# A graph attention layer: the third key form summed on VectorE and GpSimd instead of TensorE

## The reference

```
h = relu(layernorm(x));  mx = masked_x
S = (mx @ Wlq) @ (h @ Wlk).T / 16;  S = where(adj, S, -1e9)
g = (mx @ Wgq) @ (mean(h) @ Wgk).T / 16;  e = mx @ Wes
m = max(rowmax(S), g, e);  den = sum(exp(S - m)) + exp(g - m) + exp(e - m)
res = exp(S-m)/den @ (h @ Wlv + blv) + exp(g-m)/den * (mean(h) @ Wgv + bgv)
      + exp(e-m)/den * (mx @ Wev + bev)
out = x + max(res, mx)
```

## Time and profile before

| | |
|---|---|
| median of 3 runs | 729.83 us (729.6 to 729.88) |
| the profiled execution | 729.67 us, its span 727.8 us |
| PE, matmuls | 721.6 us busy, 99% |
| PE, weight loads | 513.1 us, 70% |
| DVE | 566.9 us, 78% |
| ACT | 532.3 us, 73% |
| POOL | 433.2 us, 60% |
| granted TensorE clock | 1.0 of full speed over the span |

### The profile page before, as it was taken

One profiled execution on the slowest core, in us unless ns is written; L12 is line 12 of the kernel. 1 busy time (PEld: TensorE's weight loads), 2 busy tenths in 40 slices (PEclk: granted clock), 3 DMA queues, 4 the chain that ended last, 5 costly groups with the idle time before them and its releaser, 6 DMA issues.

```text
span 727.8 us, 15215 instructions
## 1 busy us (share of the span) xinstructions
PE 721.6 (99%) x5344; PEld 513.1 (70%) x5344; DVE 566.9 (78%) x1349; ACT 532.3 (73%) x709; POOL 433.2 (60%) x300
## 2 busy tenths in 40 slices
PE   8999999999999999999999999999999999999998
PEld 7677566667766777676767676676777776676798
DVE  6975988777887797878887887878878787876545
ACT  6885967858677777776878687678767777777690
POOL 4779889455465455556545655565556545644584
PEclk9999999999999999999999999999999999999999
DMA  9783777869779888988878797989888798888797
GB/s 301 133 179 76 161 154 150 158 136 215 159 158 177 171 157 150 205 156 173 171 166 159 153 205 138 193 159 180 172 168 163 148 209 148 176 172 178 137 183 152
DMA packets 364764, 121.93 MB, mean 168 GB/s; under 512 B 324752, under 2 KB 364688, under 8 KB 364688
## 3 DMA queue, kind: packets, MB, share of 16 engines
q1 hardware_dynamic: 364144, 120.44, 81.8%
q10 hardware_dynamic: 544, 0.52, 0.2%
HBM read 36.57 MB, written 4.19 MB: 56 GB/s over the span
## 4 chain that ended last, share of the span: by engine, by line
PE 87%; POOL 3%; issue 3%; DVE 3%; ACT 2%; DMA 1%; DVEq 0%; SPq 0%; POOLq 0%; ACTq 0%
PE ps_u L1153 13%; PE ps_u L1157 13%; PE ps_u L1155 13%; PE ps_x L1031 7%; PE ps_x L1029 7%; PE ps_x L1030 7%; PE ps_q L953 4%; PE ps_v L1029 3%; PE ps_v L1031 3%; PE ps_v L1030 3%; POOL p_base L627 2%; PE ps_w L1029 2%; PE ps_w L1030 2%; PE ps_w L1031 2%; PE ps_q L1219 1%
## 5 line engine op out<-in xcount | busy, mean ns | idle before, releaser
L627 POOL TENSOR_TENSOR p_base<-s,p_base 128x1024 f16<-128x1024 f32 x112 | 242.3, 2164 | 229.1 <-ACT p_base L830 224.4
L1155 PE MATMUL ps_u<-v_rows,pT_base 128*128 128x256 f16 x944 | 257.3, 273 | 0.0
L1157 PE MATMUL ps_u<-v_rows,pT_base 128*128 128x256 f16 x944 | 257.3, 273 | 0.0
L1153 PE MATMUL ps_u<-v_rows,pT_base 128*128 128x256 f16 x944 | 257.3, 273 | 0.0
L793 ACT ACTIVATE bias<-adj,big 128x1024 f32<-128x1024 uint8 x127 | 156.5, 1236 | 130.8 <-DVE bmax L1522 128.9
L806 ACT ACTIVATE s<-s,negm,invc 128x1024 f32<-128x1024 f32 x128 | 157.0, 1226 | 8.8 <-DVE negm L1578 8.8
L830 ACT ACTIVATE p_base<-s 128x1024 f16<-128x1024 f32 x122 | 129.0, 1057 | 4.8 <-DMA pT_base<-p_base 0.9
L1153 PEld LDWEIGHTS ps_u<-v_rows,pT_base 128*128 128x128 f16 x944 | 92.3, 98 | 52.0
L1155 PEld LDWEIGHTS ps_u<-v_rows,pT_base 128*128 128x128 f16 x944 | 92.4, 98 | 51.9
L1522 DVE CUSTOM_DVE_ANT_0 s<-ps_x,bias 128x512 f32<-128x512 f32 x128 | 87.3, 686 | 47.1 <-PE ps_x L1031 43.0
L1157 PEld LDWEIGHTS ps_u<-v_rows,pT_base 128*128 128x128 f16 x944 | 92.4, 98 | 10.7
(11 more groups left out here) (255 smaller groups left out, 1315.4 us busy)
## 6 DMA issues: line engine op xcount, KB each, us to landing
adj<-adj SPq DMA_DIRECT2D x64, 256.0 KB, 3.2
pT_base<-p_base SPq DMA_TRANSPOSE x234, 3.2
s<-x SPq DMA_DIRECT2D x7, 512.0 KB, 7.9
f32q<-mx SPq DMA_DIRECT2D x14, 256.0 KB, 3.6
xm<-x SPq DMA_DIRECT2D x14, 256.0 KB, 3.0
xm<-mx SPq DMA_DIRECT2D x14, 256.0 KB, 3.6
out<-t_sb SPq DMA_DIRECT2D x14, 256.0 KB, 2.6
mxT_f<-mxT SPq DMA_DIRECT2D x4, 256.0 KB, 3.1
```

Source lines behind the costliest of these rows:

```text
L627: nc.gpsimd.tensor_tensor(p_rows(u)[:, 1], s32[:, p % NS, u % 2], p_rows(u)[:, 0], ALU.subtract).then_inc(s_plo, 1)
L1153: nc.tensor.matmul(acc, turn[:, 0, j], v_rows[:, kc, 0:D], start=opens, stop=False, skip_group_check=True)
L1155: nc.tensor.matmul(acc, turn[:, 0, j], v_rows[:, kc, D:2 * D], start=False, stop=False, skip_group_check=True)
L1157: done = nc.tensor.matmul(acc, turn[:, 1, j], v_rows[:, kc, 0:D], start=False, stop=end, skip_group_check=True)
```

## The change

`eye16`, its making on ACT, `keys_t3_sum`, `keys_t3_high` and `keys_t3_low` go. Two new functions of the same name `keys_t3` make the same sums from the float16 blocks in SBUF, with the float32 scratch `tw[:, 0]` that POOL's other key forms used before: an addition, two subtractions, the rounding to float16 and the subtraction of the rounded part, five instructions of 128x512 each. The first stands on DVE for groups 0 and 1, in periods 10 and 11. The second stands on POOL for groups 2 and 3, in its periods 12 and 14. The waits of PE that guarded `ps_q` and `eye16` go too; `p7`'s wait for T3 of its group stays.

```diff
-        eye16 = sb("eye16", [P, 2, P], F16)
...
+            def keys_t3(g):
+
+                pool.wait_ge(s_p7, PC - NG + g + 1)
+                pool.wait_ge(s_t3, g)
+                forms(twv[:, 0], plain(g, 1, 1, 0), plain(g, 1, 1, 1), ALU.add)
+                forms(twv[:, 0], twv[:, 0], plain(g, 0, 1, 0), ALU.subtract)
+                forms(twv[:, 0], twv[:, 0], plain(g, 0, 1, 1), ALU.subtract)
+                split(twv[:, 0], plain(g, 0, 1, 0), plain(g, 0, 1, 1), s_t3)
...
                     keys_t4((p - 3) // 2)
+                if p in (PC, PC + 2):
+                    keys_t3((p - PC) // 2 + 2)
...
-            act.wait_ge(s_const, 4)
-            for k in range(2):
-                nc.scalar.activation(eye16[:, k], ident, ACT.Copy, scale=1.0 - 2.0 * k).then_inc(s_eye, 1)
...
-                if p in (PC - 2, PC):
-                    keys_t3_high(p - PC + 2)
-                    keys_t3_high(p - PC + 3)
...
-                if n == PC // NG + 1:
-                    pe.wait_ge(s_t3, NG)
...
-            def keys_t3_sum(g):
-
-                if g < 2:
-                    pe.wait_ge(s_qf, PC - 3)
-                else:
-                    pe.wait_ge(s_c2, 2)
-                for k, (c, hl) in enumerate(((1, 0), (1, 1), (0, 0), (0, 1))):
-                    last = nc.tensor.matmul(ps_q[:, g % 2, :], eye16[:, 1 - c], plain(g, c, 1, hl), start=k == 0,
-                                            stop=k == 3)
-                last.then_inc(s_t3sum, 1)
...
                         for b in range(2):
-                            if p == PC - 2 and t:
-                                keys_t3_sum(b)
                             classic(p, t, b)
...
-                    if p == PC:
-                        keys_t3_sum(2)
-                        keys_t3_sum(3)
...
-            def keys_t3_low(g):
-                dve.wait_ge(s_t3hi, g + 1)
-                nc.vector.tensor_tensor(plain(g, 0, 1, 1), ps_q[:, g % 2].rearrange("p (j q) -> p j q", q=P),
-                                        plain(g, 0, 1, 0), ALU.subtract).then_inc(s_t3, 1)
+            def keys_t3(g):
+
+                dve.wait_ge(s_t4, NG)
+                dve.wait_ge(s_p7, PC - NG + g + 1)
+                if g:
+                    dve.wait_ge(s_t3, g)
+                at = tw[:, 0].rearrange("p (j q) -> p j q", q=P)
+                nc.vector.tensor_tensor(at, plain(g, 1, 1, 0), plain(g, 1, 1, 1), ALU.add).then_inc(s_t3sum, 1)
+                for hl in range(2):
+                    dve.wait_ge(s_t3sum, 4 * g + hl + 1)
+                    nc.vector.tensor_tensor(at, at, plain(g, 0, 1, hl), ALU.subtract).then_inc(s_t3sum, 1)
+                dve.wait_ge(s_t3sum, 4 * g + 3)
+                nc.vector.tensor_copy(plain(g, 0, 1, 0), at).then_inc(s_t3sum, 1)
+                dve.wait_ge(s_t3sum, 4 * g + 4)
+                nc.vector.tensor_tensor(plain(g, 0, 1, 1), at, plain(g, 0, 1, 0), ALU.subtract).then_inc(s_t3, 1)
...
                     out12(p)
+                    if p == PC - 2:
+                        keys_t3(0)
...
                     out22(p)
-                    if p == PC - 2:
-                        keys_t3_low(0)
-                        keys_t3_low(1)
+                    if p == PC - 1:
+                        keys_t3(1)
...
                         add12(p)
-                    if p == PC:
-                        keys_t3_low(2)
-                        keys_t3_low(3)
```

More of the change, by code:

```diff
@@ L221, in build @@
         s_t1, s_t2, s_t4, s_t3, s_tw = (sem(n) for n in ("s_t1", "s_t2", "s_t4", "s_t3", "s_tw"))
-        s_t3sum, s_t3hi, s_eye = (sem(n) for n in ("s_t3sum", "s_t3hi", "s_eye"))
+        s_t3sum = sem("s_t3sum")
         s_bias = sem("s_bias")
@@ L830, in p_high @@
                 nc.scalar.activation(p_rows(u)[:, 0], s32[:, p % NS, t], ACT.Copy).then_inc(s_phi, 1)
-            def keys_t3_high(g):
-                act.wait_ge(s_t3sum, g + 1)
-                nc.scalar.activation(plain(g, 0, 1, 0), ps_q[:, g % 2].rearrange("p (j q) -> p j q", q=P), ACT.Copy
-                                     ).then_inc(s_t3hi, 1)
             def mean_rows():
@@ L1160, in p_times_v @@
                         done.then_inc(s_pv, 1)
-            def keys_t3_sum(g):
-                if g < 2:
-                    pe.wait_ge(s_qf, PC - 3)
-                else:
-                    pe.wait_ge(s_c2, 2)
-                for k, (c, hl) in enumerate(((1, 0), (1, 1), (0, 0), (0, 1))):
-                    last = nc.tensor.matmul(ps_q[:, g % 2, :], eye16[:, 1 - c], plain(g, c, 1, hl), start=k == 0,
-                                            stop=k == 3)
-                last.then_inc(s_t3sum, 1)
             def es_values(n):
-                if n == 0:
-                    pe.wait_ge(s_t3, 2)
                 if n < QH:
@@ L1279, in _ @@
                 if b == NB - 1:
-                    pe.wait_ge(s_eye, 2)
                     pe.wait_ge(s_gev, 3)
```

## The result

The changed kernel takes **732.23 us** (median of 5 runs, 731.73 to 733.32) where the kernel before takes 729.73 (5 runs, 729.47 to 729.88): a ratio of 1.0037, with a 95% interval of 1.0026 to 1.0048. It is slower by 0.37%, more than the 0.2% that a measurement of this kernel can tell from none. Forecast were 734.4 and slower; the range, 727.2 to 736.6, holds the time. The profiled execution took 733.22 us, with a span of 731.4.

What follows compares the result with a forecast made beforehand. TensorE's matmuls cover 99% of the span, but from period 13 to 19 a ring of VectorE, ScalarE and GpSimd sets the pace. Sum: -3.45 + 3.45 + 3.2 + 1.4 = +4.6 us, so 734.4 us, range 727.2 to 736.6.

Steps and rivals of the forecast that it cites:

- TensorE's 3.45: Periods 10 and 12: 16 matmuls at 0.215 us go, taking 3.45 us of work off TensorE.
- VectorE's string to `add11(12)`: Periods 10 and 11: VectorE's added forms and blocks by GpSimd make `p6(12)` start at about 149.9, 1.7 us later.
- The ring's 3.2 at `out12(13)`: Periods 12 and 13: the pace-setting ring of VectorE, ScalarE and GpSimd gets 3.2 us late, bounds 1.2 to 4.4.
- `keys_t3(3)`'s 1.4: Period 14: GpSimd's 6.0 us form where it idled 4.62 makes `p_low(20)` and `p_low(21)` 1.4 us later.
- The gain kept: Rival, chance 0.18: VectorE's ten instructions mostly slip between GpSimd's, `add11(12)` done by 145.9; 727.6 to 726.4 us.
- Even: Rival, chance 0.22: part of the lead survives at `p6(12)`, and GpSimd's forms take it back; 729.8 give or take 1.4.
- More lost: Rival, chance 0.10: both `p_low` block, `row_max` meets three instructions, the lag reaches `p7(15)`; 5.8 + 1.4, 737 us.
- (1): Sign in the changed profile: TensorE has a gap of several microseconds before `p6(12)`, released by `add11`.
- (2): Sign: VectorE's `keys_t3` instructions much longer than 0.68 us in two or three places, each ending with one of GpSimd's.
- (3): Sign: the steps of `row_max` around 155 us take over 1 us each.
- (4): Sign: `p_low(20)` on GpSimd has no idle time before it.
- (5): Sign: TensorE's next gaps stand in periods 14 to 19, before `p5`, released by `out12`.

Runs made afterwards that it cites:

- e3: Changed kernel with all four forms left out, VectorE's and GpSimd's, an instruction of two elements signalling in their place: 725.52 us, ratio 0.9947.
- e5: Changed kernel with `keys_t3(0)` moved behind `out22(10)`: 732.53 us, ratio 1.0040.
- e4: Changed kernel with ten idle matmuls of 128x512 into a free bank just ahead of `p6(12)`: 731.81 us, ratio 1.0031.
- e1: Changed kernel without GpSimd's two forms (groups 2 and 3): 731.94 us, ratio 1.0033, six runs in two clusters.
- e2: Changed kernel without VectorE's forms (groups 0 and 1): 726.93 us, ratio 0.9966.
- e10: Changed kernel with groups 0, 1 and 3 summed on TensorE and only group 2 on GpSimd: 728.08 us, ratio 0.9981.
- e8: Groups 0 and 1 on TensorE, 2 and 3 on GpSimd, group 3's three additions one period earlier, against the changed kernel: 728.29 us, ratio 0.9983 to before.
- e11: Changed kernel without VectorE's forms, each of GpSimd's two forms replaced by memsets that read nothing: 727.75 us, ratio 0.9974.
- e9: Changed kernel with each of VectorE's ten instructions given one operand in PSUM and two inputs, values junk: 727.91 us, ratio 0.9977.
- e6: Changed kernel with groups 0 and 1 summed on TensorE as before the change, 2 and 3 on GpSimd: 728.30 us, ratio 0.9984.
- e7: Changed kernel with groups 0 and 1 kept on VectorE, groups 2 and 3 summed on TensorE as before the change: 731.81 us, ratio 1.0032.

## Why the prediction was right and wrong

**TensorE's 3.45: right.** `e3` shows 3.4 at `p6(12)` and 3.65 to 4.0 at the end.

**VectorE's string to `add11(12)`: right, by a sum of parts that were each a little off.** Forecast were `out22(11)` ended at 143.0, `add11(12)` at 149.1 and `p6(12)` at 149.9, 1.7 late; measured are 143.8, 149.40 and 150.13, 1.96 late. `keys_t3(0)` lost about 4.0 us to `p_low(11)` and the next, where 2.8 were put; `keys_t3(1)` lost 1.0 to `mx_low(4)`, where 1.1 were. The rounding takes 0.43 us, not the 0.68 that the sum used. The estimate of about 0.3 less per group, which the prediction drew from the Trainium skill (VectorE: DVE Perf Modes, Mode 2×_2P), is borne out by the row: 0.43 against 0.69.

What was not seen is that TensorE waits in three places. The change puts five instructions ahead of `out21(10)` and `out22(10)`, whose banks TensorE's product at 135.78 wants. For the time this is nothing, since the last wait decides; `e5` removes the first gap and the time doesn't fall.

**The ring's 3.2 at `out12(13)`: this step failed.** In `e4`, the change without the fall of the clock, `out12(13)` starts at 166.19, 1.44 later than the 164.75 of before. Two things were put too high. `row_max` was to lose 3.6 us and lost 1.5 there (0.74 and 1.08 for two steps of 0.16), in the profiled changed kernel 1.0. (The 4.8 us that the forecast draws from it does not come out of its terms either: 1.7 at `p6(12)` and 3.6, less the idle time of 0.26, are 5.0.) And "one block of 2.1 us" behind `out11(13)`, by `p_low(17)`, did not come: from `out11(13)` to `out12(13)` the kernel before takes 1.69 us, `e4` 1.70, the changed one 1.71. `out11(13)` is late along with everything else, so `p_low(17)` has ended when its small followers run. The error was to move one engine's instructions by their lateness and leave the other's where the trace of before had them. The rows had shown that such an instruction, when it meets one of GpSimd's, loses the whole of it; they did not show that it will meet one. In the profiled execution the lateness at `out12(13)` is 2.69; the 1.25 above `e4` are the clock.

The path was another as well. In `e4`, `out12(12)` comes 3.23 late and so does `p_low(16)` (160.26), which ends at 162.39, 2.1 us before `out11(13)` starts. 3.23 is less than the 3.9 that the forecast had to spare: by its path, through the mask and `p_low(16)`, `out11(13)` would not be late at all. It is 1.43 late because `add22(13)` waits for TensorE, and TensorE is late since `p6(12)`. Timeline of VectorE, the first row before, the others `e4` (`q_rows` in period 13, `add22(13)` ahead of it, `out12(13)`):

```profile
159.78 2.08 DVE L1444 TENSOR_TENSOR cqs<-cq,mu 128x2 f32<-128x2 f32 x1
...
159.78 0.69 DVE L1545 TENSOR_TENSOR bias<-ps_v,bias 128x512 f32<-128x512 f32 x1 [0.60 <-PE ps_v L1026]
...
161.11 1.30 DVE L1413 TENSOR_TENSOR rtrue<-rmax,mu 128x2 f32<-128x2 f32 x1
...
166.19 0.69 DVE L1502 CUSTOM_DVE_ANT_0 s<-ps_v,bias 128x512 f32<-128x512 f32 x1
```

`add22(13)` is 1.93 late (157.85 before). `q_rows` behind it is held up for 1.1 us by `p_low(16)`, where before it was held up for 1.9 by `p_low(17)`, and so 0.8 of the 1.93 is won back; some 0.3 is lost again in idle time that shows no releaser. The block that the forecast added was in the trace of before already, ahead of `out11(13)`.

**`keys_t3(3)`'s 1.4: right in size.** `e4` less `e1` at a clock of 1.000 gives 1.3 at `p5(19)` (222.29 against 220.99) and 1.0 by the times (731.81 against 730.77), `e2` less `e3` 1.4 at the end, all for both of GpSimd's forms together; `p_low(20)` follows the form after 0.16 us of idle time, and `e10` shows that taking this form off shortens the stretch between `p6(12)` and `p5(19)` by 1.35. That it comes from GpSimd's length is what `e8` and `e11` leave standing.

**The sum.** +1.44 at `out12(13)` and +1.3 would be 2.7; `e4` has 2.47 at `p5(19)` and 2.3 at the end. Read from TensorE the 2.47 are 1.92 at `p6(12)` and, in `e4`, gaps of 0.47 and 0.84 before `p5(15)` and `p5(19)` where one of 0.91 stood. The runs of the changed kernel with a clock of 1.000 have 2.35 in the middle (732.08 - 729.73). Forecast were 4.6. Of the 2.25 us between that and the forecast 1.8 are the failed step (3.2 for 1.44); the rest is 0.1 at `keys_t3(3)` and some 0.4 of lateness that TensorE's gap at `p5(19)` and the stretch behind it took up. In the profiled execution the change is 3.55 us (733.22 against 729.67), nearer the forecast, but by the fall of the clock, a cost that the forecast did not have.

**The rivals.** The gain kept: fallen, since VectorE's blocks do not slip between GpSimd's; `e9` shows the world in which they would, at 727.91, near its 727.6. Even: no lead was left at `p6(12)`, so it had nothing to give back. More lost: one of its three parts came, `keys_t3(0)` was held up by both `p_low`; `row_max` did not lose all three steps, and no lag reached `p7(15)`.

**What was to show it.** (1), the gap before `p6(12)` released by `add11`: there, with 2.41 us and not the whole of 5. (2), long `keys_t3` instructions ending with GpSimd's: there, 3.23 us for two, 2.50 for one and 2.26 for two. (3), the steps of `row_max` over 1 us each: one of three. (4), `p_low(20)` with no idle time before it: there, 0.16. (5), gaps in periods 14 to 19 before `p5`: there but small, 0.18 at `p5(15)` and 0.83 at `p5(19)`, the latter no longer than before (0.91).

## What to carry to other kernels

What an engine loses by a change to its neighbours is read from what each of its instructions will meet, and everything that is late has to be moved together before one looks what meets what: a block that was seen in one place of the trace is a price, not a forecast that it will be paid. Work that is taken off TensorE at 99% pays only if its new home lets the next wait end as early as before; here VectorE, with 2.6 and 2.3 us of idle time just there, reached TensorE's wait 5 us later than without this work, 1 for the work and 4 for being held up, because both its inputs lay in SBUF beside a busy GpSimd. The same forms were worth having where nobody waited for the engine: on GpSimd in period 12, with groups 0 and 1 left to TensorE, for 728.1 to 728.3 us in all. GpSimd's form in period 14 brought nothing beyond that (`e6` against `e10`).

## What the runs showed of the hardware that was not expected

**TensorE's clock fell behind short gaps, in some executions and not in others.** In the changed kernel three gaps of 1.79, 1.08 and 2.41 us end at 135.78, 143.97 and 150.13 us, and behind the third the granted clock is 0.50 for 3.4 us in the profiled execution; two runs of five show it in their mean clock, and it costs 1.2 to 1.4 us. In `e1`, with nearly the same gaps (1.64, 0.98, 2.41), it is three runs of six, and 2.3 us; the profiled one is of those without. In `e5` it is five of five, behind one gap of 3.50. In `e4`, with 1.78, 0.97 and then ten matmuls, none of six; and in `e7`, with 1.62, 0.96 and 1.36, none of five. What decides within one kernel between a run with it and one without stays open. A median over such runs can jump by 2 us between two clusters.

**An operand in PSUM frees VectorE from GpSimd.** Instructions of 128x512 take 0.69 to 0.71 us beside `p_low` with one input in PSUM, where those with both inputs in SBUF took up to 2.5.

**Beside GpSimd's memsets it is the other kind that waits.** In `e11` a step of two inputs took 0.16 us beside them, a step of one input up to 0.51 (another of its kind, at 155.71, took 0.17). Timeline of VectorE in `e11`:

```profile
155.51 0.16 DVE L1411 TENSOR_TENSOR rtrue<-rmax,mu 128x2 f32<-128x2 f32 x1
...
155.91 0.51 DVE L1418 TENSOR_SCALAR cq<-rclamp 128x2 int32<-128x2 int32 x1
```

**Left open.** Whether the first groups' forms would cost less in a period in which GpSimd is idle was not tried: a form is written over a block that `p7` reads until then, and a second place for it would be needed. Nor was it followed up where the 0.2 to 0.6 us of `e3` beyond TensorE's 3.45 come from.
